# Channel-major partitions, whole-tile saves, norm strips, residual round column groups, and later raw statistics in a wavelet and 5x5-similarity kernel

## The reference

```python
x = x + _L0_conv_ref(_gn(x), L0_conv_w0, L0_conv_w1, L0_conv_w2, L0_conv_bias)
x = x + _L1_conv_ref(_gn(x), L1_conv_spatial_weight)
```

```python
dot = jnp.einsum('bchw,bckhw->bkhw', x, patches)
norm_x = jnp.sqrt(jnp.sum(x * x, axis=1))
norm_p = jnp.sqrt(jnp.sum(patches * patches, axis=1))
sim = dot / jnp.maximum(norm_x[:, None] * norm_p, EPS)
weight = (sim + 1.0) * 0.5 * spatial_weight[None, :, None, None]
out = jnp.einsum('bckhw,bkhw->bchw', patches, weight)
```

## Time and profile before

| what | value |
|---|---|
| time, median of 3 runs | 2235.41 us (2229.73 to 2240.69) |
| the profiled execution: time, span | 2231.01 us, 2229.3 us |
| TensorE, mean granted clock | 0.885 of full |
| busy: PE, DVE, ACT, POOL | 78%, 61%, 33%, 19% of the span |
| DMA queues: SP's, POOL's | 33.5% and 17.6% of 16 engines' span |

### The profile page before, as it was taken

The page is one execution under the profiler, slowest core; times in us unless marked ns, Lnnn a source line. Parts: engine busy times, 40 slices in busy tenths (PEclk is TensorE's granted clock), DMA queues, the critical chain, the costliest instruction groups (busy, mean ns, idle before and its releaser), DMA issues.

```text
span 2229.3 us, 53057 instructions
## 1 busy us (share of the span) xinstructions
PE 1737.3 (78%) x19007; PEld 988.9 (44%) x19007; DVE 1363.9 (61%) x1995; ACT 742.9 (33%) x1318; POOL 430.6 (19%) x760
## 2 busy tenths in 40 slices
PE   5776887978878787878778787878779787876576
PEld 3542344545444444535345344545345444443354
DVE  6427756756677456856577456755578465865453
ACT  2320243423333243423333243423333252423341
POOL 1343322012311123012310123012300224010000
PEclk7888897889989898989989898999989898987577
DMA  5243337552666337562656447552754447571555
GB/s 164 75 106 95 85 104 174 151 137 78 187 155 159 94 104 191 153 140 78 179 156 151 97 114 196 152 139 79 176 149 128 117 105 201 127 174 38 141 145 127
DMA packets 128073, 296.57 MB, mean 133 GB/s; under 512 B 44532, under 2 KB 77300, under 8 KB 127220
## 3 DMA queue, kind: packets, MB, share of 16 engines
q1 hardware_dynamic: 90864, 190.39, 33.5%
q0 software_dynamic: 36864, 101.47, 17.6%
HBM read 221.92 MB, written 69.83 MB: 131 GB/s over the span
## 4 chain that ended last, share of the span: by engine, by line
PE 41%; DMA 17%; DVE 15%; SPq 13%; issue 10%; ACT 2%; DVEq 1%; POOL 1%; ACTq 0%; POOLq 0%
PE conv L1274 11%; DMA unit_mem<-d_n 8%; DMA d_n<-st_n 8%; PE conv L1248 6%; PE gram L1339 5%; PE out_ps L1364 5%; PE out_ps L1375 3%; SPq L409 3%; PE conv L1233 3%; PE stat_ps L1297 3%; SPq L383 3%; SPq L402 2%; SPq L381 2%; PE vals_ps L1322 2%; PE conv L1484 2%
## 5 line engine op out<-in xcount | busy, mean ns | idle before, releaser
L1012 DVE SCALAR_TENSOR_TENSOR wgt<-gram,tapw 124x512 f32<-124x512 f32 x512 | 350.1, 685 | 476.9 <-PE gram L1339 441.2
L1274 PE MATMUL conv<-thl,wconv 128*128 128x496 f16 (+2 forms) x1920 | 535.5, 407 | 20.0 <-DVE xa L892 10.7
L454 POOL DMA_DIRECT2D ring<-in_x x576 | 334.1, 585 | 666.5 <-ACT xa L526 345.0
L1339 PE MATMUL gram<-unit_mem 128*60 128x128 f16 x4096 | 250.6, 247 | 210.1 <-DMA unit_mem<-d_n 137.9
L1339 PEld LDWEIGHTS gram<-unit_mem 128*60 128x60 f16 x4096 | 152.3, 113 | 420.0 <-issue 419.5
L1274 PEld LDWEIGHTS conv<-thl,wconv 128*128 128x128 f16 x1920 | 167.3, 103 | 215.3 <-issue 62.1
L1248 PE MATMUL conv<-thl,wconv 128*128 128x480 f16 (+7 forms) x1200 | 256.9, 368 | 0.0
L483 POOL DMA_DIRECT2D up<-d_z x128 | 68.5, 537 | 813.1 <-DVE xa L943 755.4
L1297 PE MATMUL stat_ps<-st_sq,sq_c 128*128 128x306 f32 x256 | 117.9, 549 | 125.5 <-DVE flag L993 40.4
L1375 PE MATMUL out_ps<-wgt,vals 124*32 124x128 f32 x4096 | 204.8, 296 | 0.8 <-DVE wgt L1012 0.4
L526 ACT ACTIVATE vals<-vals_ps 124x512 f32<-124x512 f32 x128 | 76.2, 596 | 341.3 <-PE vals_ps L1322 337.6
(11 more groups left out here) (137 smaller groups left out, 2110.8 us busy)
## 6 DMA issues: line engine op xcount, KB each, us to landing
unit_mem<-d_hl SPq DMA_DIRECT2D x128, 360.0 KB
unit_mem<-d_hl SPq DMA_DIRECT2D x256, 180.0 KB
ring<-in_x POOLq DMA_DIRECT2D x288, 128.0 KB, 3.4
ring<-in_x POOLq DMA_DIRECT2D x288, 127.0 KB, 3.7
d_hl<-st_hl SPq DMA_DIRECT2D x128, 180.0 KB
d_v<-st_v SPq DMA_DIRECT2D x128, 180.0 KB
unit_mem<-d_v SPq DMA_DIRECT2D x64, 360.0 KB
up<-d_z POOLq DMA_DIRECT2D x160, 128.0 KB, 4.9
```

What stands on the lines that cost most here:

```text
L454: pool.dma_start(dst, src).then_inc(raw_in[slot], 16)
L1012: V.scalar_tensor_tensor(out=dst, in0=g, scalar=SIM_SCALE ** 2, in1=tapw[:, :].unsqueeze(1).to_broadcast([KN, 2, 2 * QN]), op0=ALU.add, op ...
L1274: last = mm(dst[:, :, b0:b1], wconv0[:, w, 2 * (p % ROWS4) + s, dx + 2, :], thl[:, p % 2, d, s, :, b0 + dx:b1 + dx] if p % ROWS4 != 1 else ...
L1339: last = mm(bank[row:row + KQ, col:col + QN], key[:, q, e_at, TH * KW * g:TH * KW * g + KQ], tile[:, :, TH * g + 1:TH * g + 1 + TH, 1:1 + ...
```

## The change

The diff makes the partitions channel-major (`4*c + q`), so a save can address all 128 partitions in one dimension; it does each of the unit and value saves with one DMA instead of two. The norms are stored already cut into four strips (`st_s`, 720 elements instead of 612), so their save has 16 short rows and their load two DMAs instead of four. `st_n` has one buffer instead of two; the wait for save `h - 2` moves from the first norm copy to the copy of the values on ACT and to the third step of the refinement on DVE. The residual's loops are swapped, quadrant outside and column group inside, and its stationary operand takes every fourth column of `ident`. Raw statistics 0 to 3 move from the head to unit 0, 4 to 7 from unit 0 to unit 1, and the group norm's small steps one unit later. On POOL, the `z1` store and `load_up(0)` go ahead of statistics chunks 4 to 7, and `load_up(1)` ahead of split chunks 0 to 3. The mean added at the output is spread over partitions by four small matmuls a batch.

```diff
-SAVES, LOADS = 80, 176
+SAVES, LOADS = 48, 144
...
-                mix[4 * c + t, C * q + c] = 0.5 * haar[t, q]
-                gather[C * q + c, t, C * t + c] = 0.5
+                mix[4 * c + t, 4 * c + q] = 0.5 * haar[t, q]
+                gather[4 * c + q, t, 4 * c + t] = 0.5
...
-                for hl in range(2):
-                    sp.dma_start(d_hl[b, h, hl].rearrange("c q n -> q c n"), st_hl[:, hl, h % 2, :]).then_inc(half_saved[h % 2], 16)
-                for hl in range(2):
-                    sp.dma_start(d_v[b, h, hl].rearrange("c q n -> q c n"), st_v[:, hl, h % 2, :]).then_inc(half_saved[h % 2], 16)
-                sp.dma_start(d_n[b, h], st_n[0:P:C, h % 2, :]).then_inc(half_saved[h % 2], 16)
+                sp.dma_start(d_hl[b, h].rearrange("l c q n -> (c q) l n"), st_hl[:, :, h % 2, :]).then_inc(half_saved[h % 2], 16)
+                sp.dma_start(d_v[b, h].rearrange("l c q n -> (c q) l n"), st_v[:, :, h % 2, :]).then_inc(half_saved[h % 2], 16)
+                sp.dma_start(d_n[b, h].rearrange("e q n -> q e n"), st_s[0:Q, h % 2, :].rearrange("p (e n) -> p e n", e=GROUPS)).then_inc(half_saved[h % 2], 16)
...
-                norms = d_n[b, u].rearrange("(a q) (h w) -> a (q h) w", a=1, w=SW)
-                for e in range(GROUPS):
-                    row = 64 + C * (e // 2)
-                    sp.dma_start(norm_strips[s][row:row + 1, e % 2].rearrange("a (n w) -> a n w", w=KW),
-                                 norms[:, :, TW * e:TW * e + KW]).then_inc(unit_in[s], 16)
+                for a in range(2):
+                    row = 64 + C * a
+                    sp.dma_start(norm_strips[s][row:row + 1].rearrange("p e (q n) -> p (e q) n", q=Q),
+                                 d_n[b, u, 2 * a:2 * a + 2].rearrange("(p e) q n -> p (e q) n", p=1)).then_inc(unit_in[s], 16)
...
-                    dst = ring[C * q:C * q + C, slot, :].rearrange("p (h w) -> p h w", w=IMG)[:, :, 0:IMG - cp]
+                    dst = ring[q:P:Q, slot, :].rearrange("p (h w) -> p h w", w=IMG)[:, :, 0:IMG - cp]
...
-                    raw_for_stats(i + 1, nxt, range(SLOTS, CHUNKS))
                     pool.wait_ge(z1_done, 2 * i + 2)
                     pool.dma_start(d_z1[i], z1[:, :, :].rearrange("p h w -> p (h w)")).then_inc(z1_saved, 16)
                     pool.wait_ge(z1_saved, 16 * i + 16)
                     load_up(i, 0)
+                    raw_for_stats(i + 1, nxt, range(SLOTS, CHUNKS))
+                    load_up(i, 1)
                     raw_for_split(i + 1, nxt, range(SLOTS))
-                    load_up(i, 1)
...
-                    act.wait_ge(half_saved[h % 2], START + SAVES * (4 * b + h // 2))
...
                     copy(st_b[:, :], st_a[:, :], func=ACT.Square).then_inc(root_squared, 1)
+                    act.wait_ge(half_saved[h % 2], START + SAVES * (4 * b + h // 2))
...
-                prep_chain.link(dve, V.scalar_tensor_tensor(out=sq, in0=sq, scalar=EPS_SIM ** -0.5, in1=st_a[:, :],
-                                                            op0=ALU.mult, op1=ALU.mult))
+                dve.wait_ge(half_saved[h % 2], START + SAVES * (4 * b + h // 2))
+                prep_chain.link(dve, V.tensor_tensor(in_strips(st_s[:, h % 2, :]), strips(st_n[:, :]), strips(st_a[:, :]), ALU.mult))
...
-                    raw_stats(i + 1, 0)
-                    raw_stats(i + 1, 1)
                     level1_out(i, 0)
...
-                    raw_stats(i + 1, 2)
-                    raw_stats(i + 1, 3)
...
-                            if k < 4 and j == 0:
-                                raw_stats(i + 1, SLOTS + k)
+                            if k < 4 and j < 2:
+                                raw_stats(i + 1, SLOTS * j + k)
...
-                for g in range(BANDS):
-                    row = BH * r + TH * g
-                    for q in range(Q):
-                        last = mm(o[C * g:C * g + C, q, :].rearrange("p (h w) -> p h w", h=TH), ident[:, C * q:C * q + C],
+                for q in range(Q):
+                    for g in range(BANDS):
+                        row = BH * r + TH * g
+                        last = mm(o[C * g:C * g + C, q, :].rearrange("p (h w) -> p h w", h=TH), ident[:, q:P:Q],
                                   x1[:, row:row + TH, UW * half:UW * (half + 1)], start=False, stop=False)
...
+                            for g in range(BANDS):
+                                last = mm(stat_ps[C * g:C * g + C, 0:1], average[:, 0:P:Q], mean_conv, start=True, stop=True)
+                            last.then_inc(mean_out, 1)
```

More of the change, by code:

```diff
@@ L113, in host_constants @@
             for q in range(Q):
-                mix[4 * c + t, C * q + c] = 0.5 * haar[t, q]
-                gather[C * q + c, t, C * t + c] = 0.5
+                mix[4 * c + t, 4 * c + q] = 0.5 * haar[t, q]
+                gather[4 * c + q, t, 4 * c + t] = 0.5
     part = np.arange(P)
-    average = np.where(part[:, None] % C == part[None] % C, 0.25, 0).astype(np.float32)
-    same_quadrant = (part[:, None] // C == part[None] // C).astype(np.float32)
+    average = np.where(part[:, None] // Q == part[None] // Q, 0.25, 0).astype(np.float32)
+    same_quadrant = (part[:, None] % Q == part[None] % Q).astype(np.float32)
     square = np.stack([mix, average, same_quadrant, np.eye(P, dtype=np.float32)], 1)
@@ L245, in build @@
         d_v = dram("d_v", [B, 2 * BANDS, 2, C, Q, FN], F16)
-        d_n = dram("d_n", [B, 2 * BANDS, Q, UN], F32)
+        d_n = dram("d_n", [B, 2 * BANDS, GROUPS, Q, SN], F32)
         passed = sem("passed")
@@ L368, in _ @@
             for q in range(Q):
-                sp.dma_start(small[C * q:C * q + C, 6:7], bias.rearrange("(c a) -> c a", a=1)).then_inc(const_in, 16)
+                sp.dma_start(small[q:P:Q, 6:7], bias.rearrange("(c a) -> c a", a=1)).then_inc(const_in, 16)
             sp.dma_start(spat[:, :], spatial.rearrange("(a k) -> a k", a=1).to_broadcast([P, TAPS])).then_inc(const_in, 16)
@@ L642, in count_own @@
                 act.wait_ge(unit_low, START + 8 * b + h)
-                nc.scalar.activation(st_hl[:, 1, h % 2, 0:UN], st_n[:, h % 2, :], ACT.Sign, bias=edge[:, :], scale=-1.0,
+                nc.scalar.activation(st_hl[:, 1, h % 2, :], st_s[:, h % 2, :], ACT.Sign, bias=edge[:, :], scale=-EPS_SIM ** -0.5,
                                      accum_out=short[:, h % FLAGS:h % FLAGS + 1]).then_inc(short_kept, 1)
@@ L701, in iteration @@
                 for j in range(CONV_TILES):
-                    if conv and j == 2:
+                    if conv and j == 3:
                         root(gn1, gn1_var, gn1_root, i + 1)
@@ L777, in set_live @@
                     dve.wait_ge(unit_out, START + 8 * (i - 1))
-                V.tensor_copy(mean_ls, mean_conv).then_inc(live_set, 1)
+                if first(i):
+                    V.tensor_copy(mean_ls, mean_conv).then_inc(live_set, 1)
+                else:
+                    dve.wait_ge(mean_out, i)
+                    V.tensor_copy(mean_ls, stat_ps[:, 0:1]).then_inc(live_set, 1)
                 dve.wait_ge(live_set, i + 1)
@@ L992, in set_flag @@
                 pads = PAD_EDGE if h // 2 in (0, BANDS - 1) else PAD_INNER
-                V.tensor_scalar(flag[:, h % FLAGS:h % FLAGS + 1], stat_ps[0:1, 0:1], 0.5, float(P * UN // 2 - pads), ALU.mult, ALU.add)\
+                V.tensor_scalar(flag[:, h % FLAGS:h % FLAGS + 1], stat_ps[0:1, 0:1], 0.5, float(P * FN // 2 - pads), ALU.mult, ALU.add)\
                     .then_inc(flag_done, 1)
@@ L1077, in iteration @@
                         alone(dve)
-                        short_ones = dve.value_load(flag[0:1, j % FLAGS:j % FLAGS + 1], min_val=0, max_val=P * UN)
+                        short_ones = dve.value_load(flag[0:1, j % FLAGS:j % FLAGS + 1], min_val=0, max_val=P * FN)
                     for k in range(PAIRS):
@@ L1437, in hook @@
                                 alone(pe)
-                                short_ones[0] = pe.value_load(flag[0:1, j % FLAGS:j % FLAGS + 1], min_val=0, max_val=P * UN)
+                                short_ones[0] = pe.value_load(flag[0:1, j % FLAGS:j % FLAGS + 1], min_val=0, max_val=P * FN)
                                 unit_here(b, j)
@@ L1455, in hook @@
                                 if k == 7:
-                                    count_short(b, j + AHEAD, i + 2 if conv_on and j == 1 else None)
+                                    count_short(b, j + AHEAD, i + 2 if conv_on and j == 2 else None)
                                 if k in (0, 2):
@@ L1460, in hook @@
                                 filter_group(b, j, 3)
-                        if conv_on and j == 1 and k in (4, 6):
+                        if conv_on and j == 2 and k in (4, 6):
                             if ls and k == 4:
-                                pe.wait_ge(n2_kept, START + 16 * b + 10)
+                                pe.wait_ge(n2_kept, START + 16 * b + 12)
                             gn_products(gn1, gn1_part, gn1_mm, i + 1, k // 5)
```

(10 more changed lines are left out.)

36 lines of the change are left out of this document (18 added, 18 removed).

## The result

| what | before | after |
|---|---|---|
| time, median | 2234.03 us (2229.73 to 2240.69) | 2014.64 us (2011.4 to 2025.32) |
| ratio, 95% interval | 1 | 0.9024, 0.8983 to 0.9064 |
| profiled execution: time, span | 2231.01, 2229.3 us | 2011.4, 2009.7 us |
| mean granted clock | 0.885 | 0.908 |

The change takes 219 us or 9.8% off the time; forecast were 2055 us and 180 us less. The prediction had the sign, the main mechanism (saves that confine themselves to a few DMA engines make loads late) and the likeliest case; the gain was 39 us larger, and it came in part from other places than forecast.

What follows compares the result with a forecast made beforehand. PE bounds the kernel where nothing is late, DVE close behind in units 0 to 4; saves and loads cause lateness. Gains of 188 us less 8 of costs give 180 less: 2055 us, range 2005 to 2100, with two rivals 1990 to 2125.

Steps and rivals of the forecast that it cites:

- the likeliest case: The forecast itself, 2055 us for the whole kernel, with its own range of 2005 to 2100; chance 0.62.
- Saves: SP's queue: save 0 down some 6 us after its first issue, 5 earlier; three issues take 2.7 us.
- The wait before unit 6: PE's 11.5 us idle before unit 6 shrinks to 1: 74 us less, plus 6 in unit 6 from the clock.
- Unit 0: First unit of an iteration: 1.1 us less of 3.2 us PE idle, 8 us in all.
- the copies of point 0: ACT's copies in unit 0 no longer wait for the `z1` store: 1.1 us each time, 8 us in all.
- Unit 1: Second unit: 25.2 us instead of 28.2 despite 2.7 us more DVE statistics work, 21 us less in all.
- Head: Start of each iteration: two flags come earlier without raw statistics before them, 1.1 us each, 15 us less.
- Residual: PE's residual matmuls go from 77 to 48 ns a record, 59 us less over 64 units, 42 counted.
- rival 2: Residual no faster, its pace set by weight loads or writes to one bank: 42 us more, 2097 us; chance 0.12.
- Iteration 8: Last iteration, no convolution hiding transfers: load waits 16 us less, save 0 6 us less, together 22.
- Costs: DVE's longer third step, 6.7 us, ACT's sign count and four tiny matmuls a batch: together 8 us more.
- rival 3: Slower: POOL's ring and `up` transfers, writing every fourth partition, spread badly over DMA engines; 2320 us at factor 4; chance 0.03.

Runs made afterwards that it cites:

- the longer list: Changed kernel with nine DMAs a save instead of three and four norm DMAs a load, rows of 720 bytes kept: 2040.44 us, ratio 0.9127 to the kernel before.

## Why the prediction was right

The forecast time was right, but in part by luck: large errors of its terms cancel. The table has every stretch of iterations 1 to 7, added up, from DVE's copy of the mean (the start of the head) and DVE's first weights of each unit, and iteration 8. Beside it stands what I had forecast, with the residual's 0.93 or 0.4 us added to its unit.

| stretch | before, us | after, us | gained | forecast |
|---|---|---|---|---|
| head | 438.8 | 439.6 | -0.8 | 15 |
| unit 0 | 189.3 | 133.0 | 56.3 | 8 + 6.5 = 14.5 |
| unit 1 | 198.8 | 159.6 | 39.2 | 21 + 2.8 = 23.8 |
| units 2 to 4 | 473.0 | 456.2 | 16.8 | 8.4 |
| unit 5, the wait, unit 6 | 326.9 | 249.6 | 77.3 | 74 + 6 + 13 = 93 |
| unit 7 | 147.0 | 140.1 | 6.9 | 6.5 |
| iteration 8 | 192.1 | 168.0 | 24.1 | 22 + 5.3 = 27.3 |
| costs | | | in the above | -8 |
| sum | | | 219.8 | 180.5 |

Against the forecast, units 0 to 4 gave 66 us more and the other stretches 34 us less; the 8 us of costs, which lie within the stretches, I had taken off besides. This is an account of two executions; the experiments isolate only the saves, the residual, the longer list, the statistics and the save wait.

**Saves: right, and more than forecast.** I had scaled the `z1` store and expected 6 us from save to load; it was 3.9. From the first issue to the end of the third went 1.4 us against my 2.7, because a DMA of twice the rows was not between half a pair and a whole pair, 0.75 to 1.5 us, but 0.40. The Trainium skill ("DMA: Bandwidth & Descriptors", section "Why a DMA increments its semaphore by 16 and not by 1") says the number of engines is the largest up to 16 that divides the outermost sizes on both sides. Four quadrants outermost give four of sixteen, and the trace agrees: a share of 0.21 before, where four of sixteen are 0.25, and of 0.53 after, more than four can give.

**The wait before unit 6: right, with a smaller gain around it.** I kept 1 us of 11.5, and no wait for a load was left. Units 5 and 6 with it gained 11.0 us an iteration, where my terms and the residual's share had 13.3. Shown by the experiments is that the cut of the save alone does half of the change, and that about 5 us of SP's issue time are worth 22 us more. My working put the fewer issues into the moment of landing and did not price them by themselves.

**Unit 0: the term that was most mis-sized.** I took 1.1 us for the copies of point 0 and 0.9 for the residual; it gained 8.0 an iteration. I had read 3.2 us of idle from iteration 5, which had one of the shortest units 0, and I put the granted clock at nothing here. Over the seven iterations PE's idle fell from 40.1 to 16.7 us, and its busy time on the same matmuls from 149.2 to 116.3 us, of which the residual's order explains 10. The mean granted clock was 0.86 before and is 1.00 now. In iteration 5 PE had been busy 1.4 of the 3 us that begin 9 us ahead of unit 0's weights and 1.5 of the last 3, and the next 3 us had a clock of 0.66, partly the lower of the two levels; in the changed kernel it is busy 2.3 to 2.4 in the same two and the clock stays at 1.00. No run tests that the one brings the other.

**Unit 1: mis-sized.** I took 3 us and the residual's 0.4; it gained 5.6. DVE was busy 21.3 us, near the 22.1 I had worked out, but in iteration 5 it idled 1.4 us and not the 3.1 that I took from unit 2: of unit 2's 4.1 us of idle 3.1 were waiting for PE, not a cost of DVE's own. The statistics' work on unit 1 was right in size and hurt less.

**Head: no net gain.** I gave the flags 15 us, and the heads gained none. PE's counts, which wait for the first flag, did wait less in the seven iterations, 4.6 us instead of 11.2. In iteration 5 the head, before and after, was:

```profile
1278.40:1339.50 61.10, 51.60 (x277) 28.49 (x275) 35.01 (x55) 29.43 (x52) 16.79 (x29) 0.99 0.42 113
...
1169.00:1232.20 63.20, 55.74 (x280) 31.07 (x279) 33.48 (x52) 29.70 (x52) 11.95 (x21) 0.94 0.50 133
```

PE waits less there and works longer on nearly the same matmuls. Over the seven heads its idle fell by 13 us (69.3 to 55.8), near the 15, and its busy time rose by 14 (369.6 to 383.8), at a mean granted clock of 0.94 instead of 0.96, which by this ratio would be 9 of the 14. The profile of the kernel with statistics undone, 17 us longer in its heads, speaks for the term too, with one execution each. The step that failed is that an earlier flag counts in full while the clock stays as it was; why the clock is lower stays open.

**Residual: the mechanism right, the size near by luck.** I took the filter sums' average of 48 ns a record, 59 us less in all, and let 42 of them count. The new order ran at 77.6 us / 2048 = 38 ns; it took 91 us of busy time away, and about half of it counts: undoing it costs 49 us by the ratios, and alone it brings 43. Why the filter sums go more slowly in the same order no run shows. The rule of the Trainium skill on 16-byte lines ("SBUF — State Buffer", section "Door 1: The DMA port swizzle") showed in the load (142 against 114 ns) and not in the sum. The rule of the Trainium skill on row groups ("TensorE: Matmul & The Clock Gate", section "The mechanism"), my rival 2, did not hold for these matmuls, which use all rows and go round the column groups: 73 to 78 us of busy time instead of 169.

**Iteration 8: about right.** 24 us less against 22, or 27 with the residual's share.

**Costs: right in size, unseen in the sum.** DVE's third step takes 908 ns instead of 796, and ACT's count 892 instead of 801. POOL's queue has 17.5% instead of 17.6% of the engines, so rival 3 had nothing behind it.

## What to carry to other kernels

Look at a transfer's share of the DMA engines while it runs alone: here a store at a third of the share of another (0.21 against 0.63) had four quadrants outermost, and re-cutting it, a change of four lines, brought 5.1%. Read a stretch in every iteration and not in one, and read its granted clock: unit 0, forecast from one iteration's idle, gained four times as much. When loads come in time, the next wait in the order of the program takes over (here a flag that shares a bank), and two swapped lines there gave more than moving a whole group of statistics. Try small float32 matmuls that fill one column group each in an order that goes round the groups; it took more than half of their busy time away here, and half of that reached the end.

## What was not expected of the hardware

A store DMA of 128 partitions by two rows took 0.40 us to issue, a pair with quadrants outermost 1.49 us for the same rows, and a DMA of 72 rows of 40 bytes 0.9 to 1.0 us: in these cases the time to issue follows the shape, not the bytes. Matmul records of 128 columns came 36 to 38 ns apart round the column groups although each weight load took 114 to 142 ns.
